# Reordered slots and PSUM banks in a software-pipelined transformer kernel, with the input loaded first

## The reference

```python
x = x + 0.5 * ffn_stack(layernorm(x))   # 6 layers
x = x + mid_block(layernorm(x))         # one linear-attention block with an MLP
x = x + 0.5 * ffn_stack(layernorm(x))   # the same 6 layers again
# one layer of the stack:
q, k, v = split(shift_tokens(x) @ Wqkv)          # 16 heads of 64
q = rotary(l2norm(q) * q_scale); k = rotary(l2norm(k) * k_scale)
sim = 8 * q @ k.T                                # windows of 32 tokens, this window and the one before
x = softmax(mask(sim)) @ v @ Wo + x
a, gate = split(layernorm(shift_tokens(x)) @ W1 + b1)   # 341 each
x = (a * gelu(gate)) @ W2 + b2 + x
```

## Time and profile before

| what | us |
|---|---|
| runs, median of 3 (lowest, highest) | 3683.65 (3676.86, 3694.67) |
| profiled execution, its own time | 3676.91 |
| profiled execution, span | 3674.8 |
| PE busy with matmuls | 3319.7 |
| GpSimd, VectorE, ScalarE busy | 2723.6, 2812.9, 2512.2 |

### The profile page before, as it was taken

One profiled execution on the slowest core, in us unless ns is written; L12 is line 12 of the kernel. 1 busy time (PEld: TensorE's weight loads), 2 busy tenths in 40 slices (PEclk: granted clock), 3 DMA queues, 4 the chain that ended last, 5 costly groups with the idle time before them and its releaser, 6 DMA issues. The chain is left out here.

```text
span 3674.8 us, 152254 instructions
## 1 busy us (share of the span) xinstructions
PE 3319.7 (90%) x64040; PEld 2512.8 (68%) x64040; DVE 2812.9 (77%) x4959; ACT 2512.2 (68%) x3080; POOL 2723.6 (74%) x2152
## 2 busy tenths in 40 slices
PE   6899999999999999998677999999999999999996
PEld 4777777777777777776336777777777777777774
DVE  4888878877888878886447878878788888788883
ACT  4777777777777777775126777777777777777773
POOL 5887887887887887784008878788788878878771
PEclk8999999999999999999789999999999999999998
DMA  3332332332332232332002333333332332332221
GB/s 92 80 85 76 78 83 76 80 87 74 79 88 76 76 87 74 80 86 62 6 0 72 84 77 77 84 78 78 83 80 76 82 85 74 80 87 71 72 71 29
DMA packets 207414, 272.67 MB, mean 74 GB/s; under 512 B 55700, under 2 KB 101648, under 8 KB 206736
## 3 DMA queue, kind: packets, MB, share of 16 engines
q1 hardware_dynamic: 206736, 262.94, 27.7%
HBM read 60.35 MB, written 1.05 MB: 17 GB/s over the span
## 5 line engine op out<-in xcount | busy, mean ns | idle before, releaser
L1239 POOL TENSOR_TENSOR V<-RAWQK,TAB 128x512 f32<-128x512 f32 x768 | 964.8, 1278 | 572.5 <-PE PS L338 558.9
L386 PE MATMUL PS<-WH,XH 128*128 128x512 f32 x1152 | 518.3, 450 | 46.1 <-POOL XL L1219 26.8
L1265 POOL TENSOR_TENSOR V<-V,U 128x1024 f32<-128x1024 f32 x192 | 455.0, 2370 | 28.7 <-POOL V L1239 1.7
L387 PE MATMUL PS<-WH,XL 128*128 128x512 f32 x1152 | 463.2, 402 | 2.8 <-issue 2.6
L1281 POOL TENSOR_TENSOR V<-V,U 128x1024 f32<-128x1024 f32 x192 | 454.5, 2367 | 15.2
L388 PE MATMUL PS<-WL,XH 128*128 128x512 f32 x1152 | 463.3, 402 | 0.5 <-issue 0.5
L338 PEld LDWEIGHTS PS<-EYE,V 128*128 128x128 f32 x3072 | 355.0, 141 | 103.4 <-issue 101.9
L338 PE MATMUL PS<-EYE,V 128*128 128x128 f32 x3072 | 401.0, 274 | 3.4 <-ACT PT L760 3.0
L507 PEld LDWEIGHTS PS<-OT,WO 128*128 128x128 f32 x3072 | 375.1, 193 | 20.3 <-ACT OT L779 2.9
L437 PEld LDWEIGHTS PS<-KT,QT 64*32 64x32 f32 x24576 | 278.6, 105 | 155.5 <-issue 151.2
L507 PE MATMUL PS<-OT,WO 128*128 128x128 f32 x3072 | 377.7, 276 | 2.7 <-ACT OT L779 2.2
(11 more groups left out here) (162 smaller groups left out, 7194.1 us busy)
## 6 DMA issues: line engine op xcount, KB each, us to landing
V<-VS SPq DMA_DIRECT2D x3072, 64.0 KB
ROTB<-c_rot SPq DMA_DIRECT2D x192, 128.0 KB, 2.8
WSTAGE<-wqkv SPq DMA_DIRECT2D x33, 512.0 KB, 3.9
WO<-wo SPq DMA_DIRECT2D x12, 512.0 KB, 3.8
W<-w SPq DMA_DIRECT2D x12, 341.0 KB, 3.2
QKS<-qks SPq DMA_DIRECT2D x12, 128.0 KB, 3.6
W<-w SPq DMA_DIRECT2D x12, 114.0 KB
VS<-wqkv SPq DMA_DIRECT2D x2, 512.0 KB, 4.4
```

The lines of the kernel that those rows point to most:

```text
L386: pe.matmul(o, XH[:, p, :], WH[:, w, cols], start=True, stop=False)
L387: pe.matmul(o, XL[:, p, :], WH[:, w, cols], start=False, stop=False)
L1239: ins = pool.tensor_tensor(paired(V[:, k])[:, :, :, h * half:(h + 1) * half], split(RAWQK[:, k])[:, :, :, (1 - h) * half:(2 - h) * half], ...
L1265: pool.tensor_tensor(V[:, 0], V[:, 0], U[:, 0], ALU.add).then_inc(q_turned, 1)
```

## The change

The change has five parts, all of which leave the arithmetic as it is.

1. **Another order in the slots of all engines.** The scores stand at the beginning of PE's slot and the weighing half a slot later, cut in two; 16 transposes of keys and queries lie between the halves. Keys and queries of a chunk are projected in the same slot. The output projection comes one slot later (t-4), the feed-forward matmuls one slot later (t-2), and the feed-forward steps of ScalarE and GpSimd at t-3. ScalarE's loop has 109 slots, GpSimd's 109, PE's 108. VectorE's `norm` reads sums of the slot before, so CHAIN_OFF becomes 2.
2. **Another placement of the banks**, and with it the lists in `after(...)`.
3. **x is loaded first**, in four parts with a semaphore each; the constants and the first layer's weights follow. The casts of those weights move behind the first norm on ScalarE.
4. **The norms ahead of the stacks** start group by group and use banks 0 and 2 for the spread values, with one more wait for `m_dg`.
5. `shift` waits in the first 16 chunks only for its own group.

```diff
-B_Q = 5
-B_K = 3
-B_V = 3
-B_TQ = 0
-B_TK = 3
-B_S = 0
+B_Q = 3
+B_K = 5
+B_V = 5
+B_TQ = 3
+B_TK = 0
+B_S = 3
 B_O = 5
-B_P = 3
-B_TO = 5
+B_P = 0
+B_TO = 0
...
-LAG, SEED_LAG, CHAIN_OFF, CHAINS = 7, 0, 0, 106
+LAG, SEED_LAG, CHAIN_OFF, CHAINS = 7, 0, 2, 108
...
+                if c % 4 == 0:
+                    pe.wait_ge(x_in[c // 4], 16)
...
-                for t in range(107):
-                    queries(t - 1)
-                    turn_weights(t - 3)
-                    turn_queries(t - 2)
-                    ffn_first(t - 1)
-                    turn_keys(t - 2)
-                    ffn_second(t - 1)
-                    ffn_third(t - 1)
-                    weigh_a(t - 3)
-                    weigh_b(t - 3)
-                    values(t - 1)
-                    turn_outputs(t - 3)
+                for t in range(108):
                     scores_a(t - 2)
                     scores_b(t - 2)
+                    values(t - 1)
+                    project_out(t - 4)
                     keys(t)
-                    project_out(t - 3)
+                    turn_weights(t - 2)
+                    queries(t)
+                    turn_outputs(t - 3)
+                    weigh_a(t - 2)
+                    ffn_first(t - 2)
+                    turn_keys(t - 1)
+                    turn_queries(t - 1)
+                    weigh_b(t - 2)
+                    ffn_second(t - 2)
+                    ffn_third(t - 2)
...
-            norm_all(0, lambda g: group(XR, g), xr_ready, [NG] * NG)
+            norm_all(0, lambda g: group(XR, g), xr_ready, [1, 3, 3, 4], at=(0, 2))
...
-                    if c < CH:
-                        act.wait_ge(xa_done, xa_count(inv, -1))
-                    elif c % 4 == 0:
+                    if c % 4 == 0:
                         act.wait_ge(xa_done, xa_count(inv, c // 4 - NG))
...
-                for t in range(107):
-                    keep_halo(t - 3)
-                    copy_keys(t - 1)
+                for t in range(109):
+                    copy_queries(t - 1)
+                    keep_outputs(t - 4)
                     square_keys(t - 1)
-                    exponentials(t - 3)
-                    copy_queries(t - 1)
-                    keep_weights(t - 3)
+                    ffn_early(t - 3)
+                    keep_keys(t - 2)
                     keep_queries(t - 2)
-                    ffn_early(t - 1)
                     square_queries(t - 1)
-                    keep_keys(t - 2)
-                    ffn_late(t - 1)
                     shift(t)
+                    ffn_late(t - 3)
                     keep_values(t - 1)
-                    keep_outputs(t - 3)
+                    keep_halo(t - 2)
+                    exponentials(t - 2)
+                    copy_keys(t)
+                    keep_weights(t - 2)
...
                 for t in range(111):
+                    row_sum(t - 3)
+                    sum_keys(t - 1)
                     scale_outputs(t - 3)
+                    ffn(t - 3)
+                    sum_queries(t - 1)
+                    row_max(t - 2)
                     norm(t - 1)
-                    row_max(t - 2)
+                    add_back(t - 4)
                     cos_keys(t)
-                    add_back(t - 3)
                     scale_keys(t - 1)
-                    row_sum(t - 2)
                     cos_queries(t)
-                    sum_keys(t)
-                    sum_queries(t)
-                    ffn(t)
...
-                for t in range(107):
+                for t in range(109):
+                    sin_queries(t - 2)
+                    low_part(t - 1)
                     add_keys(t - 2)
+                    add_queries(t - 2)
+                    ffn(t - 3)
+                    scale_queries(t - 2)
                     table(t)
-                    scale_queries(t - 2)
-                    ffn(t - 1)
-                    sin_queries(t - 1)
-                    add_queries(t - 1)
                     sin_keys(t - 1)
-                    low_part(t)
...
+            sp.dma_start(EYE[:, :], a["c_eye"]).then_inc(consts, 16)
+            for b in range(NG):
+                sp.dma_start(XIO[:, 4 * b:4 * b + 4, :], a["x"].rearrange("b (c p) d -> p (b c) d", p=P)[:, 4 * b:4 * b + 4, :]).then_inc(
+                    x_in[b], 16)
...
-            sp.dma_start(XIO, a["x"].rearrange("b (c p) d -> p (b c) d", p=P)).then_inc(x_in, 16)
```

More of the change, by code:

```diff
@@ L302, in _, with norm_all @@
                     mm.then_inc(xt_ready, 1)
-            def norm_all(b, rhs, ready, values, twice=False):
+            def norm_all(b, rhs, ready, values, twice=False, at=(5, 6)):
                 def variance(g):
@@ L328, in norm_all @@
                         pe.wait_ge(m_ln, n - 1)
-                    mm = pe.matmul(PS[:, 5 + n % 2, :], SPREAD[:, :], DIAGM[:, n % 2, :], start=True, stop=True)
+                    mm = pe.matmul(PS[:, at[n % 2], :], SPREAD[:, :], DIAGM[:, n % 2, :], start=True, stop=True)
                     if twice:
@@ L429, in turn_keys @@
                     pe.wait_ge(k_scaled, count(inv, c))
[L430 removed]
+                    after(use(o_kept, c - 2), use(p_kept, c - 1), third(c - 2), use(k_kept, c - 1), third(c - 3), third(c - 4))
+                    after(use(o_kept, c - 2), use(p_kept, c - 1), second(c - 2), use(k_kept, c - 1), second(c - 3), second(c - 4))
                     turn(lambda h: V[:, 1, 2 * h:2 * h + 2, :].rearrange("p r d -> p (r d)"), B_TK).then_inc(k_rows, 1)
@@ L445, in scores_a @@
                         return
-                    after(second(c + 1), use(q_kept, c), use(exp_done, c - 1), use(exp_done, c - 1), second(c - 1), second(c - 2))
-                    after(third(c + 1), use(q_kept, c), use(exp_done, c - 1), use(exp_done, c - 1), third(c - 1), third(c - 2))
+                    after(use(q_kept, c), use(uq_done, c + 1), use(exp_done, c - 1), use(exp_done, c - 1))
                     for r in range(2):
@@ L464, in turn_weights @@
                     pe.wait_ge(exp_done, count(inv, c))
-                    after(use(uk_done, c + 2), use(v_kept, c + 1), use(k_kept, c), use(p_kept, c - 1))
+                    after(third(c - 1), use(k_kept, c), use(o_kept, c - 2), use(p_kept, c - 1), third(c - 2), third(c - 3))
+                    after(second(c - 1), use(k_kept, c), use(o_kept, c - 2), use(p_kept, c - 1), second(c - 2), second(c - 3))
                     turn(lambda j: PR[:, 2 * j:2 * j + 2, :].rearrange("p r k -> p (r k)"), B_P).then_inc(p_rows, 1)
@@ L494, in turn_outputs @@
                     pe.wait_ge(o_scaled, count(inv, c))
-                    after(use(o_scaled, c), use(o_scaled, c), use(uq_done, c + 2), use(o_kept, c - 1))
+                    after(use(p_kept, c + 1), third(c), use(k_kept, c + 1), use(o_kept, c - 1), third(c - 1), third(c - 2))
+                    after(use(p_kept, c + 1), second(c), use(k_kept, c + 1), use(o_kept, c - 1), second(c - 1), second(c - 2))
                     turn(lambda h: ON[:, 2 * h:2 * h + 2, :].rearrange("p r d -> p (r d)"), B_TO).then_inc(o_rows, 1)
@@ L504, in project_out @@
                     pe.wait_ge(o_kept, count(inv, c))
-                    after(first(c + 2), use(xb_done, c - 1), first(c + 0), first(c - 1))
+                    after(first(c + 1), use(xb_done, c - 1), first(c + 0), first(c - 1))
                     for h in range(NP_):
@@ L521, in ffn_first @@
                         return
-                    after(use(xb_done, n - 3), first(n - 1), first(n - 2), first(n - 3))
+                    after(use(xb_done, n - 2), first(n - 1), first(n - 2), first(n - 3))
                     if q == 0:
@@ L667, in _ @@
             act.activation(EYEB[:, :], EYE[:, :], ACT.Copy).then_inc(cast, 1)
-            for k in range(3):
-                act.wait_ge(w_first[k], 16)
-                act.activation(WH[:, 0, k * HEADS * DH:(k + 1) * HEADS * DH], W_FIRST[k], ACT.Copy).then_inc(w_high, 1)
             for b in range(4):
@@ L848, in _ @@
             norm_all(0, 1.0)
+            for k in range(3):
+                act.wait_ge(w_first[k], 16)
+                act.activation(WH[:, 0, k * HEADS * DH:(k + 1) * HEADS * DH], W_FIRST[k], ACT.Copy).then_inc(w_high, 1)
             stack(0)
```

42 lines of the change are left out of this document (20 added, 22 removed).

## The result

The changed kernel takes 3621.99 us (median of 4 runs, 3615.97 to 3626.15) against 3682.72 us before (a median of 4 too), a ratio of 0.9832 with a 95% interval from 0.9817 to 0.9846. It is faster by 1.7%. The forecast was 3644 us, 3562 to 3722. The profiled execution has a span of 3619.1 us, where the one before had 3674.8: 55.7 us less.

A forecast was written before the change was run, and what follows sets the result against it. PE's own work was taken to set the pace, leaving its idle time to gain. Gains of -130 and costs of +90 us net -40: 3637 us against the profiled 3676.9, forecast 3644 us for the median, range 3562 to 3722.

The forecast's parts named there:

- data waits, steady: PE's waits for data in the steady stretches, mainly softmax weights behind a gelu, would shrink: -33 us (0 to -87).
- issue, steady: PE's stalls from program loading: those in the weighing should go, some in the scores: -50 us (0 to -90).
- PE's busy time in the steady parts, without the holes: Clock term: some slots with long stalls and a lower granted clock would go: -5 us (0 to -10).
- start: Before the first projection (at 38.69 us): x loaded first lets PE start at about 9: -8 us (0 to -14).
- middle: Before the second stack: the same edit of the norm's groups, no load to win: -4 us (0 to -8).
- two fills: Beginning of each stack: chunk 0 passes sooner with scores at the slot's beginning: -18 us a stack (0 to -21).
- two drains: End of each stack: the last group's feed-forward stands a slot later: +3 us a stack.
- 22 holes behind the values: PE's keys projection waits for a late values copy, twice a layer in 11 layers: 3.1 us each, +68 us (+50 to +105).
- the clock behind them: A clock dip of 1 us behind each of the 22 holes in PE's work: +22 us (0 to +30).
- The third rival: PE's loading stalls only move, so their gains of 50 and 5 us fall away: 3699 us; chance 0.20.
- the first: Rival: the window copies are late for no one, +5 instead of +90: about 3559 us; chance 0.20.
- VectorE did not become the bound: Rival: VectorE's fixed row lengthens each slot; at 0.5 us over 192 slots about 3740 us; chance 0.20.

The follow-up runs named there:

- the kernel with the later load: Changed kernel, with SyncE loading WSTAGE behind the window copies of chunks 3, 7, 11 instead of 1, 5, 9: 3510.22 us, ratio 0.9523 to the kernel before.
- The cut alone: Kernel before, only the weighing's first half moved ahead of the feed-forward matmuls, which then lie between the halves: 3670.51 us, ratio 0.9971.
- the kernel with LAG 6: The kernel with the later load, feed-forward steps and the thirds one slot earlier (LAG 6 for 7): 3490.17 us, ratio 0.9479 to the kernel before.
- the two cuts above: Weighing cut in the kernel before (3670.51 us); scores cut by the six values matmuls in the kernel with the later load (3613.62 us).

## Why the prediction was right, and where its sizes were off

The mechanism and its place were right, and the time lies 22 us below the forecast. The step that failed is the fills and drains, and the terms of the steady part were sized too small on both sides. That the sum came so close is in part luck, since errors of both signs met in it. Term by term, for the profiled executions:

| step | predicted | measured |
|---|---|---|
| data waits, steady | -33 | -53 |
| issue, steady | -50 | -78 |
| PE's busy time in the steady parts, without the holes | -5 | -37 |
| start | -8 | -3.6 |
| middle | -4 | -5 |
| two fills | -36 | -17 |
| two drains | +6 | +21 |
| 22 holes behind the values | +68 | +80 |
| the clock behind them | +22 | +38 |
| sum | -40 | -55 (spans: -55.7) |

The measured numbers of the first three rows and the last two come from the waits inside the steady stretches, and from PE's busy time there: 1486.81 + 1489.28 before, 1491.19 + 1485.55 after, and 1468.94 + 1470.06 in the kernel with the later load, which has no holes.

**The holes.** Each step of the chain came as predicted: 22 of them, in the one shown the split's end 9.0 us into the slot (9.4 predicted), the load right behind it, the late copy of the values, PE at the keys. They are not alike, as I had them at 3.1 us each: 1.1 to 5.6, 3.6 on average. In the one shown, of 4.5, what was too small is the length of SyncE's window copies. From first to last issue they took 504.73 - 492.29 = 12.4 us, not 10.3, since two of them took 2.91 and 1.21 us. Why these are long no run tells. The clock behind a hole costs 1.7 us, not 1.

**The data waits.** The hand placement left the exponential 0.8 us late behind a gelu; it is 0.66 us, as the wait of PE in most such slots. The joints of VectorE and GpSimd to which I gave the rest of the 1.2 us cost little: there remain 2 x 14 us for PR, and 11 us for everything else.

**The loading of the program.** That the stalls are the loading was read from sizes alone. The trace of the kernel before bears it out: each of the 113 stalls inside the scores and the weighing ends 1.1 to 1.6 us after a packet of the instruction queue has landed, and 2.2 to 3.0 us after that packet began; of random moments of the steady parts 7% lie so behind one. A packet holds 256 records, and a block of 128 matmuls with their weight loads, 256 records too, runs in 1.6 us. So the rule taken from the blocks' length was right, and its gain at the upper end. What the prediction left out is the price of a cut: it was costed at nothing. The cut alone wins 41.5 us of issue and gives back 29.7 us of busy time. In the changed kernel the weighing's own row shows it (L474, 336.4 us for 300.4), but PE's sum does not, because the scores' row fell (303.0 for 325.0), the change also put the transposes of keys and queries into one block of 16 (L340, V: 371.3 us for 401.0), and the clock dips behind the long stalls went. Which of these made how much of the -37 us was not tried one by one. The third rival, by which the stalls would stay, is excluded: 0.4 us are left in the weighing. The Trainium skill ("Runtime: NRT & Kernel Launch", "Instruction fetch mechanics") has the loading "mostly hidden"; the measurement decides against it for such blocks, with 112.2 us at one line where the block was whole.

**Fill and drain.** This is the step that failed. I took the whole gain of the earlier scores, 18 us a fill, and 3 us a drain. But PE's idle time in a fill, the 21 us of which I took 18 as won, fell by 2 only (20.6 to 18.8 us in the first, 19.7 to 17.6 in the second): in the first the wait for XL fell from 12.6 to 4.6 us, and others came, for VS 3.7, for the scaled keys 2.5 and for QT 2.2. For the rest, moving the scores from the end of PE's slot to its start shifts work from before them to behind them: PE's busy time in the first fill fell from 71.1 to 66.0 us and that in the first drain rose from 34.5 to 43.5. The feed-forward's later slot, for which I gave the drain 3 us, costs 5.1 and 5.8 us, as the kernel with LAG 6 shows. Together the four pieces became 4 us longer, not 30 shorter.

**The start.** PE did begin at 8.54 for 14.00, 5.5 us sooner, and the first projection came 3.6 us sooner. VectorE's slow instructions beside GpSimd cost 4.7 us, which I did not see coming: the casts' move put GpSimd's split beside VectorE's norm. Another 2.8 us came back behind the norm; I put them down to the groups' own signals, which no run tries alone.

**The other rivals.** The copies were late, so the first is out. VectorE did not become the bound: the kernel without the holes runs 3499.4 us with VectorE busy 2799.9 us, 80%. The 2 us a slot that I left it in the prediction do not fit the figures beside them: 17.5 less 14.1 is 3.4, and 2 is what a slot of 16.0 us without idle time leaves.

## What to carry to other kernels

A step that is moved takes its semaphores along: ask for each engine that issues in order, above all the one that only issues DMAs, what stands behind its wait; here 22 waits for a buffer that nobody needed yet cost 112 us, and one number in the loop of loads took them away. Count a hole in TensorE's work at more than its length: here 3.6 us of waiting had 1.7 us of slower matmuls behind it. And count work across fill, steady part and drain together, since a step that is moved inside a slot may only pass it from the one to the other.

## What the runs showed of the hardware

- A long run of tiny matmuls is stopped by the loading of instructions: all 113 stalls in such runs of the kernel before end 1.1 to 1.6 us after an instruction packet has landed. With 64 + 64 matmuls, 17 others between them, there were 0.4 us of stalls in the weighing, with 128 in one piece 112.2 us. With only two to four others between them, in the kernel before, 13.9 us stayed.
- A cut in such a run costs PE 0.17 us in the run itself, though each matmul takes as long as before.
- Matmuls of 64 rows that alternate between the halves of the array, and between two PSUM banks, overlap better than those that stay in one half and one bank: 300.3 us against 430.5 us for the same 24,576. Of the difference a cut makes some 33 us, by the two cuts above. Which of half and bank it is was not separated.
- Behind a hole of 4.5 us in TensorE's work the granted clock was 0.57 for 4 us, and a matmul took 0.63 us for 0.40. The 22 holes of 3.6 us had 1.7 us of this each.
- VectorE's small instructions with both operands in SBUF took up to ten times as long while GpSimd worked beside it (1.77 us for 0.18) and ended with GpSimd's instruction of the moment, and one with an operand in PSUM did not.
